# First stage of a window-attention and gating kernel: one list of steps per engine, two low-part subtractions on GpSimd, two biases as matmuls

## The reference, cut to what matters

```
h   = layernorm(x) * g1 + b1, rolled by (-4, -4), cut into 16 windows of 64 tokens
a   = softmax(q k^T / 4 + relative_bias + shift_mask);  o = a v        (4 heads of 16)
x1  = x + unroll(o @ proj_w + proj_b)
x2  = x1 + gelu(layernorm(x1) * g2 + b2 @ fc1_w + fc1_b) @ fc2_w + fc2_b
r   = sum over one image row of (x2 @ W_right + b_right)
out = (x2 @ (W_left + W_eq) + b_left + b_eq) * r * sigmoid(x2 @ W_gate + b_gate)
y   = layernorm(out @ W_out + b_out + x2) * ln_scale + ln_bias
```

## Time and profile before

| what | value |
|---|---|
| runs | 2911.05, 2915.53, 2917.67 us; median 2915.53 |
| profiled execution: span, first to last instruction | 2913.9 us; no time beside the span is given for it, the median of the runs lies 1.6 us above |
| first stage | 30.57 (first memset) to 957.20 (end of the last store to `tokens`): 926.6 us |
| one image in the middle of the stage | 26.65 us |
| busy in the whole span | PE 80%, DVE 76%, ACT 70%, POOL 56% |

### The profile page before, as it was taken

One profiled execution on the slowest core, in us unless ns is written; L12 is line 12 of the kernel. 1 busy time (PEld: TensorE's weight loads), 2 busy tenths in 40 slices (PEclk: granted clock), 3 DMA queues, 4 the chain that ended last, 5 costly groups with the idle time before them and its releaser, 6 DMA issues. The chain is left out here.

```text
span 2913.9 us, 84659 instructions
## 1 busy us (share of the span) xinstructions
PE 2318.3 (80%) x32732; PEld 1731.1 (59%) x32732; DVE 2210.4 (76%) x3688; ACT 2045.3 (70%) x3520; POOL 1645.1 (56%) x1370
## 2 busy tenths in 40 slices
PE   3777777777776699999934565899999999677777
PEld 1555555555554477677723464688888888544444
DVE  4677877777775688898866604788888888688886
ACT  2677777777774699999922201788888888677776
POOL 3577777777775322222166500799999998633331
PEclk9999999999998799999966656899999999799998
DMA  3211111111110000000000020000000000000001
GB/s 72 53 41 37 40 43 37 37 41 36 28 26 1 16 18 14 18 18 18 16 1 1 0 59 0 9 7 7 6 6 7 6 7 6 7 23 22 22 22 26
DMA packets 144658, 62.05 MB, mean 21 GB/s; under 512 B 118676, under 2 KB 127798, under 8 KB 144566
## 3 DMA queue, kind: packets, MB, share of 16 engines
q1 hardware_dynamic: 139565, 58.00, 9.3%
q10 hardware_dynamic: 4393, 2.77, 0.5%
q0 software_dynamic: 608, 0.01, 0.0%
HBM read 14.50 MB, written 8.39 MB: 8 GB/s over the span
## 5 line engine op out<-in xcount | busy, mean ns | idle before, releaser
L1854 POOL TENSOR_TENSOR a_prl<-a_pr,a_prh 128x896 f16<-128x896 f32 x256 | 494.6, 1948 | 54.5 <-ACT a_prh L1836 54.5
L1781 DVE TENSOR_REDUCE a_nmax<-a_ps_a 128x1 f16<-128x1024 f32 x256 | 313.2, 1224 | 58.3 <-PE a_ps_a L1885 56.5
L1198 DVE TENSOR_TENSOR a_exl<-a_ex,a_exh 128x1024 f16<-128x1024 f32 x224 | 275.8, 1260 | 30.1 <-ACT a_exh L1238 29.0
L1832 ACT ACTIVATE a_pr<-a_ps_s 128x1024 f32<-128x1024 f32 x256 | 261.9, 1024 | 32.5 <-PE a_ps_s L1900 20.3
L1898 PE MATMUL a_ps_s<-a_qx,a_kh 128*128 128x128 f16 x2048 | 252.6, 219 | 1.4 <-ACT a_pr L1832 1.1
L1900 PE MATMUL a_ps_s<-a_qm,a_kl 128*128 128x128 f16 x2048 | 252.6, 219 | 0.0
L1233 ACT ACTIVATE a_ex<-a_ps_s,a_shift 128x1024 f32<-128x1024 f32 x224 | 243.1, 1100 | 1.0 <-PE a_ps_s L1281 1.0
L2145 ACT ACTIVATE f_mixed_s<-f_ps_e,f_gates 128x64 f32<-128x64 f32 x1024 | 213.3, 426 | 41.5 <-PE f_ps_e L397 38.6
L1836 ACT ACTIVATE a_prh<-a_pr 128x896 f16<-128x896 f32 x256 | 235.9, 948 | 0.2
L114 POOL TENSOR_TENSOR a_w_hl<-a_xn,a_w_hl 128x512 f16<-128x512 f32 x32 | 36.0, 1125 | 318.7 <-ACT a_w_hl L106 318.7
L1280 PE MATMUL a_ps_s<-a_w_xT 128*128 128x512 f16 x512 | 196.9, 385 | 22.0 <-ACT a_ex L1233 12.3
(11 more groups left out here) (355 smaller groups left out, 8681.7 us busy)
## 6 DMA issues: line engine op xcount, KB each, us to landing
tokens<-in_x_dram SPq DMA_DIRECT2D x32, 256.0 KB, 2.9
bl_qg<-bl_qk_high SPq DMA_DIRECT2D x128, 64.0 KB, 2.0
bl_km<-bl_qk_high SPq DMA_DIRECT2D x256, 32.0 KB, 2.0
a_xTb<-a_w_xT SPq DMA_DIRECT2D x64, 128.0 KB
out_dram<-tokens SPq DMA_DIRECT2D x32, 256.0 KB, 2.6
bl_qg<-bl_qk_low SPq DMA_DIRECT2D x64, 64.0 KB, 2.0
bl_km<-bl_qk_low SPq DMA_DIRECT2D x128, 32.0 KB, 2.0
a_qm<-a_qx SPq DMA_DIRECT2D x64, 64.0 KB, 2.0
```

The source lines that it names most:

```text
L1198: nc.vector.tensor_tensor(exl[:, at[2]], exps(at), exh[:, at[2]], ALU.subtract).then_inc(low, 1)
L1781: nc.vector.tensor_reduce(nmax[:, g:g + 1], ps_a[:], AX.X, ALU.max, negate=True).then_inc(maxed, 1)
L1832: nc.scalar.activation(pr[:, g % RING], ps_s[:, g % 2], ACT.Exp).then_inc(exped, 1)
L1854: nc.gpsimd.tensor_tensor(prl[:, r], pr[:, r, 0:P * SPLIT], prh[:, r], ALU.subtract).then_inc(low, 1)
```

## The change

Only `stage_blocks` and the loading of two biases change.

- `STEPS` and `AHEAD` go. Every step is a function of its own with a semaphore of its own (`done[name]`), and every engine has its own list, with a lag in laps for each step (`run(step, lag)`). An image now passes through lags 0 to 8; 40 laps, of which the first 9 and the last 9 are written out and 22 are looped by pairs.
- The low parts of gelu quarters 1 and 3 go from DVE to POOL (`gelu_low1`, `gelu_low3`); quarters 0 and 2 stay on DVE. The second product keeps its three fp16 products per tile.
- proj_b and b_out become bias matmuls (`BIASES` has six names); `add_row`, `net.rows` and `x2b` go. Their two loads move from ACT's DMA queue to POOL's.
- The copy `wide_xT` goes from ACT to DVE.
- `x1`, `x2`, `y` and two `xT` tiles get two buffers; the `hl` and `xT` tiles are no longer shared between steps; the DMA semaphore of the q/k layout is split in two (`laid_high`, `laid_low`).

```diff
-BIASES = {name: ... for j, name in enumerate(("left", "gatel", "right", "fc2"))}
+BIASES = {name: ... for j, name in enumerate(("left", "gatel", "right", "fc2", "proj", "out"))}
...
+def run_images(engine, image, most, full):
+    def iteration(i, k):
+        def run(step, lag):
+            if not isinstance(i, int) or 0 <= i - lag < B:
+                step(i - lag, (k - lag) % 2)
+        image(run)
...
+                def image(run):          # DVE
+                    run(top3, 4); run(gelu_low0, 6); run(gelu_low2, 6); run(wide_centred, 5); run(norm_centred, 1)
+                    run(norm_xT, 2); run(wide_sumsq, 5); run(right_low, 7); run(inverse0, 4); run(divide0, 4)
+                    run(norm_sumsq, 1); run(qk_low, 2); run(last_sum, 8); run(gated_left, 7); run(gated, 7)
+                    run(inverse1, 4); run(last_centred, 8); run(divide1, 4); run(add_x2, 6); run(top0, 3)
+                    run(top1, 3); run(wide_xT, 5); run(last_sumsq, 8); run(gated_xT, 7); run(norm_sum, 0)
+                    run(merge_xT, 4); run(add_y, 7); run(top2, 3); run(add_x1, 4); run(wide_sum, 4); run(gate_xT, 6)
...
+                def image(run):          # ACT
+                    run(gate_tanh, 7); run(take_p3, 4); run(wide_high, 5); run(take_v, 2); run(gated_high, 7)
+                    run(last_squared, 8); run(merge_high, 4); run(norm_high, 1); run(x2_high, 6); run(exp0, 3)
+                    run(exp1, 3); run(gelu0, 5); run(gelu1, 5); run(gelu2, 5); run(gelu3, 5); run(take_p0, 3)
+                    run(exp2, 3); run(take_p1, 3); run(wide_squared, 4); run(right_high, 6); run(exp3, 3)
+                    run(norm_squared, 0); run(take_p2, 3); run(qk_high, 1)
...
+                def gelu_low1(n, p):
+                    pool.wait_ge(done["gelu1"], n + 1)
+                    nc.gpsimd.tensor_tensor(gelu_low[:, 0, 512:1024], gel[:, 0, 512:1024], gelu_high[:, 0, 512:1024], ALU.subtract)
...
+                def image(run):          # POOL
+                    run(wide_var, 4); run(last_scaled, 8); run(wide_rstd, 4); run(norm_var, 0); run(wide_normed, 4)
+                    run(norm_rstd, 0); run(wide_low, 4); run(norm_normed, 0); run(gated_low, 6); run(merge_low, 3)
+                    run(last_stored, 8); run(last_var, 7); run(x2_low, 5); run(norm_low, 0); run(last_rstd, 7)
+                    run(gelu_low1, 4); run(last_normed, 7); run(gelu_low3, 4)
...
+                def image(run):          # PE
+                    run(gated_turned, 7); run(shift1, 3); run(hidden0, 5); run(hidden1, 5); run(merge_turned, 4)
+                    run(gated_out, 7); run(score2, 3); run(project, 4); run(hidden2, 5); run(gate_turned, 6)
+                    run(hidden3, 5); run(score3, 3); run(turn_p0, 3); run(shift2, 3); run(right, 6)
+                    run(norm_turned, 1); run(turn_p1, 3); run(left, 6); run(shift3, 3); run(weigh0, 3)
+                    run(turn_p2, 3); run(weigh1, 3); run(project_qk, 1); run(gate_left, 6); run(turn_p3, 3)
+                    run(weigh2, 3); run(right_rows, 6); run(weigh3, 3); run(project_v, 1); run(contract, 5)
+                    run(score0, 2); run(score1, 2); run(wide_turned, 4); run(shift0, 2)
```

More of the change, by code:

```diff
@@ L459, in run_pairs, with reached, behind @@
         iteration(i, i)
+def reached(n):
+    return not isinstance(n, int) or n >= 0
+def behind(engine, done, n, each=1):
+    if not isinstance(n, int):
+        engine.wait_ge(done, each * (n + 1))
+    elif n >= 0:
+        engine.wait_ge(done, each * min(n + 1, B))
+def run_images(engine, image, most, full):
[4 more added lines that the diff above has]
+        image(run)
+    pairs = (B - full) // 2
+    for i in range(full):
+        iteration(i, i)
+    with engine.Fori(0, pairs) as j:
+        for k in range(2):
+            iteration(2 * j + (full + k), full + k)
+    for i in range(full + 2 * pairs, B + most):
+        iteration(i, i)
 def stage_blocks(net, x):
@@ L528, in stage_blocks @@
-        AHEAD = {"norm": 3, "score": 1, "shift": 1, "turn": 1, "weigh": 1, "windows": 1, "merge": 0, "wide": 0, "gate": -1, "last": -2}
-        LAG, GAP = AHEAD["norm"] - AHEAD["wide"], AHEAD["norm"] - AHEAD["score"]
-        FETCH = 6
+        x_loaded, mask_laid, zeroed, v_zeroed = net.x_loaded, sem("bl_mask_laid"), sem("bl_zeroed"), sem("bl_v_zeroed")
+        ln = net.norms[0]
+        done = {name: sem("bl_" + name) for name in (
+            "project_qk", "qk_high", "qk_low", "laid_high", "laid_low", "project_v", "take_v", "score0",
[4 rows of a table added]
+            "merge_xT", "project", "add_x1", "wide_sum", "wide_centred", "wide_squared",
+            "wide_sumsq", "wide_var", "wide_rstd", "wide_normed", "wide_high", "wide_low",
+            "wide_turned", "wide_xT", "hidden0", "gelu0", "hidden1", "gelu1", "hidden2",
+            "gelu2", "hidden3", "gelu3", "gelu_low3", "contract", "add_x2", "x2_high", "x2_low",
+            "gate_turned", "gate_xT", "right", "right_high", "right_low", "gate_left",
+            "gate_tanh", "right_rows", "gated_left", "gated", "gated_high", "gated_low",
+            "gated_turned", "gated_xT", "gated_out", "add_y", "last_sum", "last_centred",
+            "last_squared", "last_sumsq", "last_var", "last_rstd", "last_normed", "last_scaled",
+            "last_stored")}
@@ L691, in last @@
[L691 to L703 removed]
+                nc.vector.memset(norm_hl[:, :, C - 1:C], 1.0)
@@ L842, in _, with norm_var @@
-                run_pairs(pool, STEPS, AHEAD, {"norm": norm, "score": nothing, "shift": nothing, "turn": nothing,
-                                               "weigh": nothing, "windows": windows, "merge": nothing, "wide": wide, "gate": gate,
-                                               "last": last})
-                pool.wait_ge(stored["t"], B)
+                def norm_var(n, p):
+                    pool.wait_ge(done["norm_sumsq"], n + 1)
+                    nc.gpsimd.tensor_tensor(wn["var"], wn["ss"], net.eps[:], ALU.add).then_inc(done["norm_var"], 1)
@@ L1007, in last, with norm_turned @@
[L1007 to L1012 removed]
+                def norm_turned(n, p):
+                    pe.wait_ge(done["norm_low"], n + 1)
+                    behind(pe, done["gelu3"], n - 4)
+                    for g in range(NT):
+                        half = (g + NT - 1) % NT
+                        at = (half // 2) * 4 * WIN * WIN + (half % 2) * WIN * WIN // 2
+                        out = bank16(fb).rearrange("p (w t) -> p w t", t=WIN * WIN)[:, at // 64:at // 64 + 4, at % 64:at % 64 + 32]
+                        ins = nc.tensor.transpose(out, norm_hl[:, g], net.perm16[:, 0])
+                    ins.then_inc(done["norm_turned"], 1)
```

989 lines of the change are left out of this document (583 added, 406 removed), and 4 rows, old and new, of the table done.

## The result

The changed kernel takes 2773.27 us (median of 4 runs, 2764.26 to 2780.45), the kernel before 2913.29 us beside it (2906.31 to 2917.67). The ratio is 0.9515 [0.9491, 0.9539]: 4.85% faster, 140 us. Predicted were 2780 us.

The account below looks back on a forecast made before the run. The order of steps, not a full engine, was taken to bound the stage: 4.9 start + 645 (29 laps of 22.25) + 141 drain = 791 us instead of 926.6, a span of 2778.3, median 2780 us; range 2745 to 2830.

Parts of the forecast that it names:

- The order sets the pace, not an engine's work: Middle of the stage: no engine is full in the 26.65 us per image; reordering can win down to the fullest engine.
- POOL's work, 18.9 us: POOL per image: instructions sum to 19.36 us with two gelu low parts at 1.16; overlapping starts give back about 0.45.
- The port, 0.9 us from two stays of 0.44: Port shared by POOL and DVE: two DVE steps push between POOL steps, 0.9 us per lap; bounds 0 and 2.2.
- The turn-around, 2.45 us: POOL idles 2.45 us per lap ahead of wide_var while DVE works from wide_centred through wide_sumsq.
- The lap, 22.25: Time per image mid-stage: 18.9 + 0.9 + 2.45 = 22.25 us, bounds 20.8 and 25.2; 29 laps make 645.
- drain 141: From the last norm_sum to the stage's end: 141 us with three more laps to pass, 125.9 before.
- The other engines fit: DVE 19.9, ACT 19.4 and PE 20.9 us busy per lap, all within POOL's lap.
- Nothing in the later stages: After the stage: later stages take as long as before; releasing more semaphores costs 0 to 2 us, taken as 0.
- A: Rival: the port costs nothing and POOL's idle turn-around shrinks; lap 20.8, time 2738 us; chance 0.11.
- B: Rival: POOL is dearer, gelu low parts at 1.95 and every port stay paid; lap 25.2, 2866 us; chance 0.12.
- C: Rival: POOL waits 5 us more per lap for ACT's gelus; lap 27.25, 2925 us, slower; chance 0.03.
- D: Rival: no change, lap stays 26.5 us because the ring through banks 0 and 1 sets it; chance 0.02.

Follow-up runs that it names:

- the four corners: Old or new order of steps, with or without the three moves of work: 2914.6 (old, none), 2933.8 (old, moves), 2798.3 (new, none), 2773.3 us (new, moves).
- gelu_back_lists: Changed kernel with all gelu low parts on DVE and the lists of DVE and POOL reordered for that: 2752.4 us.
- undo_bias: Changed kernel with both bias rows (proj_b, b_out) added by POOL again, without their bias matmuls: 2763.36 us.
- both_lists: Changed kernel with DVE's and POOL's lists reordered so DVE's two-input steps meet POOL less often, no instruction added or removed: 2740.28 us.
- undo_gelu: Changed kernel with the two gelu low parts put back from POOL to DVE: 2756.91 us.
- scaled_first: Changed kernel with last_scaled put ahead of wide_var in POOL's list: 2819.74 us.
- extra_pool: Changed kernel with one more POOL instruction of 1.27 us per image, its result unused: 2811.01 us.

## Why the prediction was right

The span was to be 2778.3 us and is 2770.2, 8.1 less: 7.6 of it in the stage (791 forecast, 783.4 measured), 0.5 against it in the setup, the rest behind the stage. Its steps one by one:

- *The order sets the pace, not an engine's work*: shown by the four corners. The order alone, with all that comes with it, brings 116 us. `gelu_back_lists` points the same way: with 17.5 us of work on POOL and 19.4 on DVE the lap is 21.44, and the one long wait stands behind a step late in DVE's list.
- *POOL's work, 18.9 us*: 18.78 in the laps without the two stays. The gelu low parts on POOL, bounded by 1.11 and 1.95, take 1.16 alone.
- *The port, 0.9 us from two stays of 0.44*: the 22.09 us lap has two, on `last_xn` (0.45) and `gelu_low3` (0.44), and 19.67 - 18.78 = 0.89 in sum. It was not said that the grant can also fail to alternate; where it does, the stays go, and the gap grows by 1.21.
- *The turn-around, 2.45 us*: 2.42, ended by `wide_sumsq`, through the very steps named (0.55 for `wide_centred`, two of 0.60, then `wide_sumsq`).
- *The lap, 22.25*: 22.09 or 22.4. With 17 of the one and 6 of the other, 22.17 on average, 640.4 us are 28.9 laps; 29 were taken. Start 4.9 (4.9 measured), drain 141 (138).
- *The other engines fit*: DVE 20.7 busy in the lap and not 19.9, since its instructions held at the port count as busy; ACT 19.4 as forecast; PE 20.2 and not 20.9. The two bias matmuls add less than 0.42 to PE: it is busy 20.23 here and 20.04 in a lap of `undo_bias`, which lacks them. PE's wait for `exp3` ahead of `project_qk` is there with 26.4/23 = 1.15 us instead of 1.9.
- *Nothing in the later stages*: 1955.75 us against 1956.7, release of the semaphores included.

The drain's low clock shows again: the granted clock falls to half where PE has next to nothing to do, the lower of its two levels (1.2 of 2.4 GHz). The stage's last 10 us:

```profile
804.45:814.45 10.00, 0.01 (x1) 0.00 (x0) 3.31 (x4) 0.63 (x1) 9.21 (x8) 0.50 0.00 0
```

The rivals. A (lap 20.8 by a free port) did not come; but `both_lists` has that very lap with the same instructions, though it is not free of the port (its `last_rstd` and a low part are held): there the users of the port stand apart. B (low parts at 1.95) falls with 1.16. C (POOL waits for the gelus) falls in the new order, where POOL's `gelu_low1` follows `last_rstd` without a wait, but it is what happens to the moved steps in the old one. D (the ring through banks 0 and 1) falls, as laps of 20.8 to 21.8 pass through the same banks.

One judgement was right in the sum and wrong in its reason. I took the two moved low parts as part of the gain. In the new lists the old work takes 2798 us, the bias matmuls without the low parts 2757, the low parts without the bias matmuls 2763, both 2773 (the copy of `wide_xT` was not tried alone). Either move, with the copy, is worth 35 to 41 us, and the second one takes 10 to 16 back. Some 10 of the 35 to 41 are the laps of 24.1 at a lower clock, which only the run without either move has among these four. That `last_rstd` and DVE's block of four meet in `undo_bias`, and miss each other in the changed kernel, is seen in the timelines; that nothing else adds to the difference is not shown. The Trainium skill, "Perfetto Trace Analysis", section "Optimizing Scalar/DVE Operations", warns that a move between DVE and GpSimd might not help, since they share a port. The prediction set it aside; `undo_gelu`, 16 us faster with the low parts back on DVE, agrees with the warning.

## What to carry to other kernels

When no engine is full, price the order: follow each engine's list to the one hand-over that closes the lap, and add to POOL's work the steps between its last instruction and its next first one; that sum (18.9 + 0.9 + 2.45) gave the lap to 1%. Work moved from DVE to POOL is not free when both then ask for two SBUF operands in the same microseconds; look where DVE's two-input steps lie, and put them beside a POOL instruction that does not keep them out (here `rstd`). A step put into another engine's idle gap gains nothing if the gap is the port's turn: `scaled_first` kept its 2.42 us. And look at the granted clock of a lap before reading its length as the price of an edit: in `scaled_first` and `extra_pool` PE worked at 0.93 and was busy 1.5 us longer for the same matmuls.

## What the runs showed of the hardware

- POOL's `rstd` (128x8, 1.65 us) does not keep DVE's two-input instructions out: in `undo_bias` four of them ran at 0.68 to 0.73, two wholly and two partly beside one, and cost it 0.45 once, not four times. The Trainium skill, "SBUF — State Buffer", section "Who interferes with whom", says that a DVE instruction with two SBUF inputs contends with a GpSimd instruction that reads SBUF, and calls the lock on the shared ports exclusive; for this one the measurement differs. For the 128x512 instructions of POOL the trace agrees: DVE ends 0.55 after POOL's end.
- The port does not always alternate. With nearly the same offset (DVE asks 0.83 us after `gelu_low1` began at 370.91, 0.84 after the one at 415.40) DVE was served after one POOL instruction in the one lap and after three in the other (3.02 us). What decides it is open.
- The same matmuls take PE 20.23 us of a lap in the changed kernel and 21.75 in `scaled_first`, where the granted clock is 0.50 for the first 3 us of each lap, behind 2 us in which PE was busy for 0.13.
